# Linear attention over 16 images on one core: evictions ahead of the first exponential, statistics loads ahead of stores, one rounding and one load moved past the natural chunks, image 0 in a new order

## The chip, the cores and the metric

The kernel runs on 1 core of one Trainium2 chip. The metric is the device time of one execution in microseconds; lower is better. Five engines work side by side and meet only at semaphores: PE (TensorE, matrix products; its weight loads are listed as PEld), DVE (VectorE), ACT (ScalarE), POOL (GpSimd) and SP (SyncE), which here issues every DMA.

## The reference

`x` holds 16 images of 64 x 64 positions with 256 channels, in fp32. Each is normalized in 32 groups, goes through a linear attention whose keys get a softmax over the 4096 positions, and is added to the result.

```python
def _L0_conv_ref(x, W_qkv, W_out, b_out):
    b, h, w, c = x.shape
    n = h * w
    qkv = jnp.einsum('bhwc,cd->bhwd', x, W_qkv)
    q, k, v = jnp.split(qkv, 3, axis=-1)
    q = q.reshape(b, n, c).transpose(0, 2, 1)
    k = k.reshape(b, n, c).transpose(0, 2, 1)
    v = v.reshape(b, n, c).transpose(0, 2, 1)
    k = jax.nn.softmax(k, axis=-1)
    context = jnp.einsum('bdn,ben->bde', k, v)
    out = jnp.einsum('bde,bdn->ben', context, q)
    out = out.reshape(b, c, h, w).transpose(0, 2, 3, 1)
    return jnp.einsum('bhwc,cd->bhwd', out, W_out) + b_out

def _gn(v, G=32, eps=1e-5):
    B_, H_, W_, C_ = v.shape
    g = v.reshape(B_, H_, W_, G, C_ // G)
    m = jnp.mean(g, axis=(1, 2, 4), keepdims=True)
    s = jnp.var(g, axis=(1, 2, 4), keepdims=True)
    return ((g - m) / jnp.sqrt(s + eps)).reshape(v.shape)

x = x + _L0_conv_ref(_gn(x), L0_conv_W_qkv, L0_conv_W_out, L0_conv_b_out)
```

## The kernel before, in words

An image is cut into 8 chunks of 512 positions. Each chunk comes in twice: as `xt` with the channels on the partitions (the "transposed" chunks, `load_xt`) and as `x` with the positions on the partitions (the "natural" chunks, `load_x`). A third copy, `xs`, comes in 16 halves of 256 KB (`load_xs`) and only feeds the statistics of the normalization (`bn_half`, written `bn q` below for half q), two images ahead. Every fp32 operand of a product is split into a high part, rounded to fp32r, and a low part, the rest: ACT rounds (`xt_high`, `x_high`), and POOL subtracts (`xt_low`, `x_low`).

For each image PE makes keys, 8 chunks (`keys`, into the two halves of `ps_k`); ACT copies them out (`keys_out`, L747) and DVE keeps their running maximum (`key_maxes`, four L994 or L991 instructions a chunk). After chunks 0 to 3 and again after 4 to 7, `block_max` and `block_diag` bring the block's maxima into a diagonal, PE spreads it (`spread_max`, L506), and DVE subtracts it (`shift`, L1054). ACT makes the exponential twice (`exps`): rounded, L755, and exact, L761; `e_low` (L1061) is the difference. PE then gathers the context, chunk by chunk (`gather_high`, L542 and L544, needs `e_hi`, `x_hi` and `x_lo`; `gather_low`, L554, needs `e_lo` and frees the chunk's slots). `combine_u` and `combine_m` fold the context with the weights, and `emit` (L625, L634) makes the output, chunk by chunk in EMIT_ORDER (3, 4, 5, 6, 7, 0, 1, 2), position u, in two halves h. ACT adds the bias and writes `o_stage` (its `emit`, L795), and SP stores it.

A period of the loop works on two images: PE gathers and combines image b and makes the keys of image n = b + 1 between its emits (emit u, then keys u + 1). The order on every engine is written by hand, and each engine goes through its list in order: one waiting instruction holds all that follow. SP too has one list: its loads and stores are issued in the written order, each behind a wait for its slot, and all land through one queue. Two of these slots matter here. `o_stage` has 2, so ACT's emit of position u waits for the store of u - 2; and `ps_e` has one bank for each half, so PE's `emit(u + 1, h)` waits until ACT has taken (u, h). The first image has an order of its own, `first_gather` on DVE, and POOL makes the first POOL_LOW = 3 `e_low` of it (L398).

Of the kernel before, what the change touches and what calls it, by code (L numbers as in the profile page):

```python
# [25 lines left out]
XS_AFTER = {0: (4, 8), 2: (8, 12), 3: (12, 16)}  # L26

FIRST_XT = (8, 11, 15)
POOL_LOW = 3
# [5 lines left out]
def build(nc: bass.Bass, xt: bass.AP, xn: bass.AP, w: bass.AP, b_out: bass.AP, out: bass.AP):  # L35
# [11 lines left out]
    with ExitStack() as ctx:  # L47
# [232 lines left out]
        def _(sp):  # L280
# [45 lines left out]
            def period(b, parity, more, more2):  # L326
                for j in range(X_SLOTS, NCH):
# [13 lines left out]
                for u, j in enumerate(EMIT_ORDER):  # L341
                    if more2 or (more and j not in DOUBLED):
# [9 lines left out]
                    if more2 and u in XS_AFTER:  # L352
                        for q in range(*XS_AFTER[u]):
                            sp.wait_ge(bn_done, b * (NCH * CB) + 2 * NCH * CB + q - S_SLOTS + 1)
                            load_xs(b + 2, q)
# [8 lines left out]
        def _(pool):  # L364
# [61 lines left out]
            def period(b, parity, more, more2):  # L426
                n, np_ = b + 1, 1 - parity
                if more and b:
                    pool.wait_ge(var_parts_ready, n)
                pool.wait_ge(dm_ready, b + 1)  # L430
                if more:
                    xt_low(n, np_, 0)
                    if b:
                        rstd_of(n, np_)
                        scale_mean(n, np_)
                for j in range(HALF, NCH):
                    x_low(b, j)
                    if b == 0 and j == NCH - 2:
                        rstd_of(n, np_)
                        scale_mean(n, np_)  # L440
# [17 lines left out]
        def _(pe):  # L458
# [220 lines left out]
            def period(b, parity, more, more2):  # L679
                n, np_ = b + 1, 1 - parity  # L680
                gather_high(b, 0)
                if more and b:
                    stats_mean(n)
                gather_low(b, 0)
                gather_high(b, 1)
                if b == 0:
                    gather_low(b, 1)
                    gather_high(b, 2)
                spread_max(b, 1)
                if more and b:  # L690
                    stats_var(n)
                gather_low(b, 2 if b == 0 else 1)
                for j in range(3 if b == 0 else 2, NCH):
# [605 lines left out]
```

## Time and profile before

| | before |
|---|---|
| median of 3 runs | 1199.64 us (1195.49, 1199.64, 1200.19) |
| the profiled execution | 1202.58 us, its span 1200.6 us |
| PE busy | 1166.4 us (97%) |
| DVE busy | 931.0 us (78%) |
| ACT busy | 836.3 us (70%) |
| POOL busy | 627.0 us (52%) |
| mean DMA rate over the span | 222 GB/s |

The profiled execution took 2.9 us more than the median. The span runs from the first to the last instruction of the profiled execution. Rows of the timeline begin with start and duration in us; the idle time in brackets is what the engine waited before that instruction, with what ended it, and rows of one line close together are merged (x4 stands for four instructions, whose whole extent the duration is).

### The profile page before, as it was taken

To read this page: it belongs to the slowest core of one execution; us is meant where nothing else is said; L and a number is where in the kernel's file an instruction comes from. 1 tells how busy PE (TensorE), PEld (TensorE's weight loads), DVE (VectorE), ACT (ScalarE), POOL (GpSimd) and SP (SyncE) were. 2 spreads that over 40 slices of the span, in tenths; PEclk is the share of its full clock that TensorE was granted. 3 is DMA by queue.
4 is the path that set the end of the run, shared out by engine and by line. 5 is a ranking of instruction groups with operands and counts; after the bars stand their busy time and mean duration, and the time that the engine had idled before them with its cause. 6 is when DMAs were issued, how large, how long until landed. Compare 5 with 4: busy or idle time off the path is not lost.

```text
span 1200.6 us, 21468 instructions
## 1 busy us (share of the span) xinstructions
PE 1166.4 (97%) x8206; PEld 1089.3 (91%) x8206; DVE 931.0 (78%) x2008; ACT 836.3 (70%) x1146; POOL 627.0 (52%) x305
## 2 busy tenths in 40 slices
PE   4999999999999999999999999999999999999998
PEld 3889999989899898998989999899999989999996
DVE  6988779787796877878787797878869788796561
ACT  5667768677685776857777676776857768577764
POOL 7655563645656355553655636456463655536530
PEclk9999999999999999999999999999999999999999
DMA  8438666586766758657486665867657586573524
GB/s 318 163 134 315 228 216 236 179 296 214 258 212 202 263 188 280 228 201 250 165 316 228 215 232 179 303 212 261 214 199 271 179 295 227 198 254 119 190 84 162
DMA packets 107078, 266.70 MB, mean 222 GB/s; under 512 B 10208, under 2 KB 10208, under 8 KB 106976
## 3 DMA queue, kind: packets, MB, share of 16 engines
q1 hardware_dynamic: 106976, 265.33, 63.7%
q8 instruction: 65, 1.06, 0.4%
q14 instruction: 37, 0.30, 0.1%
HBM read 198.18 MB, written 67.11 MB: 221 GB/s over the span
## 4 chain that ended last, share of the span: by engine, by line
PE 82%; DMA 6%; DVE 4%; ACT 3%; issue 2%; POOL 1%; SPq 1%; DVEq 0%; ACTq 0%; POOLq 0%
PE ps_k L460 24%; PE ps_e L625 18%; PE ps_e L634 9%; PE ps_e L542 5%; PE ps_e L554 5%; PE ps_e L544 5%; DMA xs<-in_xt_dram 4%; PE ps_g L554 4%; PE ps_g L544 4%; PE ps_g L542 4%; PE ps_g L573 1%; PE ps_g L590 1%; DMA x_raw<-in_xn_dram 1%; DVE bn L922 1%; DVE e_raw L1054 1%
## 5 line engine op out<-in xcount | busy, mean ns | idle before, releaser
L387 POOL TENSOR_TENSOR xt_lo<-xt_raw,xt_hi 128x1024 fp32r<-128x1024 f32 x128 | 307.5, 2404 | 458.8 <-ACT xt_hi L738 194.1
L393 POOL TENSOR_TENSOR x_lo<-x_raw,x_hi 128x1024 fp32r<-128x1024 f32 x128 | 282.4, 2225 | 59.9 <-ACT x_hi L743 50.5
L994 DVE TENSOR_TENSOR mx<-ps_k,mx 128x256 f32<-128x256 f32 x480 | 203.1, 423 | 72.0 <-ACT e_raw L747 50.2
L795 ACT ACTIVATE o_stage<-ps_e,bias 128x512 f32<-128x512 f32 x253 | 168.8, 687 | 105.5 <-PE ps_e L634 101.5
L460 PE MATMUL ps_k<-wk_hi,xt_hi 128*128 128x256 f32 x1024 | 205.9, 283 | 1.4 <-DVE mx L994 1.2
L460 PE MATMUL ps_k<-wk_lo,xt_hi 128*128 128x256 f32 x1024 | 205.0, 282 | 0.0
L747 ACT ACTIVATE e_raw<-ps_k 128x512 f32<-128x512 f32 x256 | 141.2, 595 | 78.1 <-PE ps_k L460 78.1
L755 ACT ACTIVATE e_hi<-e_raw 128x1024 fp32r<-128x1024 f32 x128 | 134.8, 1053 | 67.2 <-DVE e_raw L1054 45.4
L922 DVE BATCH_NORM_STATS2 bn<-xs 128x6 f32<-128x512 f32 x240 | 153.8, 685 | 33.2 <-DMA xs<-in_xt_dram 31.9
L460 PEld LDWEIGHTS ps_k<-wk_hi,xt_hi 128*128 128x128 f32 x1024 | 164.3, 189 | 10.6 <-issue 2.4
L460 PE MATMUL ps_k<-wk_hi,xt_lo 128*128 128x256 f32 x1024 | 157.5, 282 | 0.0
L460 PEld LDWEIGHTS ps_k<-wk_lo,xt_hi 128*128 128x128 f32 x1024 | 157.1, 189 | 0.0
L625 PE MATMUL ps_e<-xt_hi,acc_hi 128*128 128x512 f32 x474 | 149.6, 397 | 4.6 <-ACT o_stage L795 4.5
L634 PE MATMUL ps_e<-xt_hi,u_lo 128*128 128x512 f32 x474 | 149.8, 397 | 0.0
L625 PE MATMUL ps_e<-xt_lo,acc_hi 128*128 128x512 f32 x474 | 149.1, 395 | 0.0
L743 ACT ACTIVATE x_hi<-x_raw 128x1024 fp32r<-128x1024 f32 x128 | 134.4, 1050 | 18.2 <-DMA x_raw<-in_xn_dram 18.2
L738 ACT ACTIVATE xt_hi<-xt_raw 128x1024 fp32r<-128x1024 f32 x128 | 135.1, 1055 | 3.8 <-DMA xt_raw<-in_xt_dram 3.7
L460 PEld LDWEIGHTS ps_k<-wk_hi,xt_lo 128*128 128x128 f32 x1024 | 137.2, 189 | 0.0
L542 PE MATMUL ps_e<-x_hi,e_hi 128*128 128x258 f32 x512 | 127.2, 286 | 2.6 <-POOL x_lo L393 2.5
L544 PE MATMUL ps_e<-x_lo,e_hi 128*128 128x256 f32 x512 | 126.5, 284 | 0.0
L542 PE MATMUL ps_g<-x_hi,e_hi 128*128 128x258 f32 x512 | 124.6, 282 | 0.0
L544 PE MATMUL ps_g<-x_lo,e_hi 128*128 128x256 f32 x512 | 124.5, 281 | 0.0
(147 smaller groups left out, 2027.6 us busy)
## 6 DMA issues: line engine op xcount, KB each, us to landing
xt_raw<-in_xt_dram SPq DMA_DIRECT2D x128, 512.0 KB, 4.6
x_raw<-in_xn_dram SPq DMA_DIRECT2D x128, 512.0 KB, 3.8
out_dram<-o_stage SPq DMA_DIRECT2D x127, 512.0 KB, 4.5
xs<-in_xt_dram SPq DMA_DIRECT2D x240, 256.0 KB, 5.0
w_setup<-in_w_dram SPq DMA_DIRECT2D x2, 256.0 KB, 9.7
out_dram<-o_stage SPq DMA_DIRECT2D x2, 256.0 KB, 2.0
wk<-in_w_dram SPq DMA_DIRECT2D x1, 256.0 KB, 10.0
wq_t<-in_w_dram SPq DMA_DIRECT2D x1, 256.0 KB, 11.0
```

What stands on the lines that cost most here:

```text
L387: nc.gpsimd.tensor_tensor(xt_lo[:, s], xt_raw[:, s], xt_hi[:, s].bitcast(F32), ALU.subtract).then_inc(xt_lo_ready, 1)
L393: nc.gpsimd.tensor_tensor(x_lo[:, s], x_raw[:, s], x_hi[:, s, :, 0:C].bitcast(F32), ALU.subtract).then_inc(x_lo_ready, 1)
L460: return nc.tensor.matmul(ps_k[:, j % 2, t // 2, (t % 2) * C:(t % 2 + 1) * C], (xt_hi, xt_lo)[xs_][:, slot(j, parity), c, t * P:(t + 1) * ...
L542: nc.tensor.matmul(ps_g[j // HALF][:, d, 0:C + 2], w_, x_hi[:, j % X_SLOTS, t, :], start=(j % HALF == 0 and t == 0), stop=False, skip_grou ...
L544: nc.tensor.matmul(ps_g[j // HALF][:, d, 0:C], w_, x_lo[:, j % X_SLOTS, t, :], start=False, stop=False, skip_group_check=True)
L625: nc.tensor.matmul(out_psum(b, u, h), hi[:, c, h * P:(h + 1) * P], x_[:, s, c, :], start=(n == 0 and c == 0), stop=False, skip_group_check ...
L634: last = nc.tensor.matmul(out_psum(b, u, h), lo[:, c, h * P:(h + 1) * P], xt_hi[:, s, c, :], start=False, stop=(c == CB - 1), skip_group_c ...
L738: nc.scalar.activation(xt_hi[:, s], xt_raw[:, s], ACT.Copy).then_inc(xt_hi_ready, 1)
L747: nc.scalar.activation(e_raw[:, j, 2 * h:2 * h + 2, :].rearrange("p t c -> p (t c)"), ps_k[:, j % 2, h, :], ACT.Copy).then_inc(k_out, 1)
L795: nc.scalar.activation(o_stage[:, u % O_SLOTS, h, :], src, ACT.Identity, bias=bias[:, h:h + 1]).then_inc(o_ready, 1)
L922: nc.vector.bn_stats(bn[:, q % CB, q // CB, :], xs[:, q % S_SLOTS, :]).then_inc(bn_done, 1)
L994: nc.vector.tensor_tensor(mx[:], tile, mx[:], ALU.max).then_inc(max_done, 1)
```

## The change

It only reorders: no instruction is added or left out, and one `e_low` of image 0 goes from POOL to DVE. Four parts belong to every period: (1) ACT takes the two output halves of position 4 ahead of the first exponentials of the next image; (2) SP issues the statistics loads ahead of the stores, and DVE takes two more of them ahead of the maxima of chunk 3, and three fewer between `block_diag` and the first `shift`; (3) ACT rounds transposed chunk 2 behind the natural chunks; (4) SP loads transposed chunk 2 of the next image behind natural chunks 4 and 5. The rest belongs to image 0.

```diff
-XS_AFTER = {0: (4, 8), 2: (8, 12), 3: (12, 16)}
-FIRST_XT = (8, 11, 15)
-POOL_LOW = 3
+XS_AHEAD = {0: (4, 8), 1: (8, 12), 2: (12, 14), 4: (14, 16)}
+FIRST_XT = (11, 13, 15)
+FIRST_X = (6, 7, 8, 9)
+POOL_LOW = 2
...
             for q in range(S_SLOTS, CB * NCH):
-                if q < 2 * X_SLOTS:
-                    load_x(0, q - X_SLOTS)
                 sp.wait_ge(bn_done, NCH * CB + q - S_SLOTS + 1)
                 load_xs(1, q)
+                if q in FIRST_X:
+                    load_x(0, FIRST_X.index(q))
...
                 for j in range(X_SLOTS, NCH):
                     sp.wait_ge(g_ps, b * NCH + (j - X_SLOTS + 1))
                     load_x(b, j)
+                    if more and b and j == X_SLOTS + 1:
+                        sp.wait_ge(e_ps, b * (CB * NCH))
+                        load_xt(n, 1 - parity, EMIT_ORDER[NCH - 1])
...
-                    if more2 or (more and j not in DOUBLED):
+                    if u < NCH - 1 and (more2 or (more and j not in DOUBLED)):
...
+                    if more2 and u in XS_AHEAD:
+                        for q in range(*XS_AHEAD[u]):
+                            sp.wait_ge(bn_done, b * (NCH * CB) + 2 * NCH * CB + q - S_SLOTS + 1)
+                            load_xs(b + 2, q)
                     if b == B - 1 and u == NCH - 1:
                         store_last()
                     elif not late(b, u, CB - 1):
                         store(b, u)
-                    if more2 and u in XS_AFTER:
...
+                if b == 0:
+                    pool.wait_ge(e_lo_ready, e_lo_count(0, HALF - 1))
...
                 for j in range(HALF, NCH):
+                    if b == 0 and j == NCH - 1:
+                        pool.wait_ge(var_parts_ready, 1)
                     x_low(b, j)
+                    if b == 0 and j == HALF + 1:
+                        xt_low(n, np_, 0)
...
+                def first_gather():
+                    gather(0, 0)
+                    gather_high(0, 1)
+                    gather_high(0, 2)
+                    gather_low(0, 1)
+                    spread_max(0, 1)
+                    gather_high(0, 3)
+                    gather_low(0, 2)
+                    gather_low(0, 3)
+                    gather(0, 4)
+                    stats_mean(1)
+                    gather(0, 5)
+                    gather_high(0, 6)
+                    stats_var(1)
+                    gather_low(0, 6)
+                    gather(0, 7)
...
             for j in range(X_SLOTS):
-                x_high(0, j)
                 keys_out(0, j, 0)
                 keys_out(0, j, 1)
+                x_high(0, j)
...
+                if b == 0:
+                    exps(0, 3)
+                    x_high(0, 4)
+                    xt_high(1, 1, 0)
+                    scales(0)
+                    for j in range(HALF, NCH):
+                        exp_high(0, j)
+                        if j < NCH - 1:
+                            x_high(0, j + 1)
+                        exp_exact(0, j)
+                    xt_high(1, 1, 1)
...
-                if more:
-                    xt_high(n, np_, 2)
                 for j in range(5, NCH):
                     x_high(b, j)
                     exps(b, j)
                 if more:
                     wk_high(n, np_)
+                    xt_high(n, np_, 2)
...
                 both_out(4)
+                emit(b, 4)
                 if more:
                     exps(n, 0)
-                emit(b, 4)
...
-            for q in range(1, 5):
+            for q in range(1, 7):
                 bn_half(1, q)
             for j in range(HALF):
                 key_maxes(0, j)
-                for q in ((5, 6), (7, 8), (9,), ())[j]:
+                for q in ((7, 8), (9, 10), (11,), ())[j]:
                     bn_half(1, q)
```

On SP, the part of a middle period that loads and stores beside the emits of positions 0 to 4 (`xt_raw` is a transposed chunk, `xs` a half for the statistics, `out_dram` a store). Before:

```order
L285 DMA xt_raw<-in_xt_dram 128x1024 [waits e_ps]
L304 DMA out_dram<-o_stage 128x2x512 [waits o_ready]
L294 DMA xs<-in_xt_dram 128x512 [waits bn_done] x4
L285 DMA xt_raw<-in_xt_dram 128x1024 [waits e_ps]
L304 DMA out_dram<-o_stage 128x2x512 [waits o_ready]
L285 DMA xt_raw<-in_xt_dram 128x1024 [waits e_ps]
L304 DMA out_dram<-o_stage 128x2x512 [waits o_ready]
L294 DMA xs<-in_xt_dram 128x512 [waits bn_done] x4
```

and now:

```order
L287 DMA xt_raw<-in_xt_dram 128x1024 [waits e_ps]
L296 DMA xs<-in_xt_dram 128x512 [waits bn_done] x4
L306 DMA out_dram<-o_stage 128x2x512 [waits o_ready]
L287 DMA xt_raw<-in_xt_dram 128x1024 [waits e_ps]
L296 DMA xs<-in_xt_dram 128x512 [waits bn_done] x4
L306 DMA out_dram<-o_stage 128x2x512 [waits o_ready]
L287 DMA xt_raw<-in_xt_dram 128x1024 [waits e_ps]
L296 DMA xs<-in_xt_dram 128x512 [waits bn_done] x2
```

The second four `xs` loads (q 8 to 11) have moved from behind the store of position 2 to ahead of that of position 1, and every store now stands behind loads that wait for DVE's statistics.

On DVE, a middle period from the maxima of chunk 2 of the next image to the first `shift` (`mx` is the running maximum, `bn` a statistics half, `e_raw<-e_raw,ps_g` the shift). Before:

```order
L922 BN_STATS bn<-xs 128x6 x4
L994 TENSOR_TENSOR mx<-ps_k,mx 128x256 x4
L922 BN_STATS bn<-xs 128x6 x4
L994 TENSOR_TENSOR mx<-ps_k,mx 128x256 x4
L1005 STREAM_TRANSPOSE turned<-mx 128x256
...
L1028 TENSOR_TENSOR u_hi<-eyes,m_parts 128x256
L922 BN_STATS bn<-xs 128x6 x4
L1054 TENSOR_TENSOR e_raw<-e_raw,ps_g 128x1024
```

and now:

```order
L968 BN_STATS bn<-xs 128x6 x4
L1040 TENSOR_TENSOR mx<-ps_k,mx 128x256 x4
L968 BN_STATS bn<-xs 128x6 x6
L1040 TENSOR_TENSOR mx<-ps_k,mx 128x256 x4
L1051 STREAM_TRANSPOSE turned<-mx 128x256
...
L1074 TENSOR_TENSOR u_hi<-eyes,m_parts 128x256
L968 BN_STATS bn<-xs 128x6
L1100 TENSOR_TENSOR e_raw<-e_raw,ps_g 128x1024
```

Two statistics halves moved ahead of the maxima of chunk 3, and one instead of four stands between the diagonal (`u_hi`) and the shift; one more now follows the maxima of chunk 4.

On DVE in image 0, from the block scales (`dm`) to the first `e_low` of the second block (`e_lo<-ps_k`). Before:

```order
L1038 TENSOR_TENSOR dm<-m_blk,m_all 32x16
L922 BN_STATS bn<-xs 128x6 x2
L1054 TENSOR_TENSOR e_raw<-e_raw,ps_k 128x1024
L1061 TENSOR_TENSOR e_lo<-e_raw,e_hi 128x1024
L922 BN_STATS bn<-xs 128x6 x2
...
L1054 TENSOR_TENSOR e_raw<-e_raw,ps_k 128x1024
L1061 TENSOR_TENSOR e_lo<-ps_k,e_hi 128x1024
```

and now:

```order
L1084 TENSOR_TENSOR dm<-m_blk,m_all 32x16
L1107 TENSOR_TENSOR e_lo<-e_raw,e_hi 128x1024 x2
L1100 TENSOR_TENSOR e_raw<-e_raw,ps_k 128x1024
L968 BN_STATS bn<-xs 128x6
L1100 TENSOR_TENSOR e_raw<-e_raw,ps_k 128x1024
L968 BN_STATS bn<-xs 128x6
...
L1107 TENSOR_TENSOR e_lo<-ps_k,e_hi 128x1024
```

Two statistics halves have left this place for the key stage, one `e_low` has come from POOL, and `take_first` (not shown) has gone behind the statistics and the `e_low` of chunk 6.

## Rows read from the trace of the kernel before

**Rows 1.** The page: busy time by engine.

```profile
PE 1166.4 (97%) x8206; PEld 1089.3 (91%) x8206; DVE 931.0 (78%) x2008; ACT 836.3 (70%) x1146; POOL 627.0 (52%) x305
```

**Rows 2.** Waits of PE's weight loads, 80 to 1150 us: released by, us, times, longest.

```profile
PEld ps_e L625 <- ACT o_stage L795: 6.2, 8, 1.8
PEld ps_e L542 <- issue: 3.1, 5, 1.0
```

**Rows 3.** Timeline, PE: start, duration; the statistics matmul, one of fifteen, once an image.

```profile
128.59 0.17 PE L517 MATMUL ps_k<-mean_parts,grp_r 128*128 128x4 f32 x1
...
566.63 0.17 PE L517 MATMUL ps_k<-mean_parts,grp_r 128*128 128x4 f32 x1
638.62 0.17 PE L517 MATMUL ps_k<-mean_parts,grp_r 128*128 128x4 f32 x1
...
1074.22 0.17 PE L517 MATMUL ps_k<-mean_parts,grp_r 128*128 128x4 f32 x1
```

**Rows 4.** Timeline of the image with the longest wait, DVE and PEld.

```profile
543.76 1.94 DVE L922 BATCH_NORM_STATS2 bn<-xs 128x6 f32<-128x512 f32 x3 [1.70 <-DMA xs<-in_xt_dram]
546.65 1.20 DVE L1054 TENSOR_TENSOR e_raw<-e_raw,ps_g 128x1024 f32<-128x1024 f32 x1
550.52 0.30 PEld L625 LDWEIGHTS ps_e<-xt_hi,acc_hi 128*128 128x128 f32 x2 [1.78 <-ACT o_stage L795]
```

**Rows 5.** The same place in the next image, DVE, ACT, PEld.

```profile
611.58 1.87 DVE L994 TENSOR_TENSOR mx<-ps_k,mx 128x256 f32<-128x256 f32 x4 [1.97 <-ACT e_raw L747]
615.54 0.42 DVE L1028 TENSOR_TENSOR u_hi<-eyes,m_parts 128x256 fp32r<-128x256 f32 x1
616.73 0.19 PEld L506 LDWEIGHTS ps_g<-u_hi,one_r 128*128 128x128 f32 x1
621.69 1.24 ACT L795 ACTIVATE o_stage<-ps_e,bias 128x512 f32<-128x512 f32 x2
622.49 0.31 PEld L625 LDWEIGHTS ps_e<-xt_hi,acc_hi 128*128 128x128 f32 x2
```

**Rows 6.** Ahead of it: DVE, SP, and one window (end: PEclk, DMA share, GB/s).

```profile
607.09 2.52 DVE L922 BATCH_NORM_STATS2 bn<-xs 128x6 f32<-128x512 f32 x4 [2.06 <-DMA xs<-in_xt_dram]
605.78 0.33 SPq L285 DMA_DIRECT2D xt_raw<-in_xt_dram  x1
609.00:610.00 1.00, 1.00 (x11) 1.00 (x10) 0.61 (x1) 0.27 (x1) 0.89 (x1) 1.00 1.07 399
```

**Rows 7.** The page, DMA issues: KB each, median us from issue to landing.

```profile
out_dram<-o_stage SPq DMA_DIRECT2D x127, 512.0 KB, 4.5
xs<-in_xt_dram SPq DMA_DIRECT2D x240, 256.0 KB, 5.0
```

**Rows 8.** A late natural chunk: ACT and POOL.

```profile
1007.56 1.06 ACT L743 ACTIVATE x_hi<-x_raw 128x1024 fp32r<-128x1024 f32 x1 [2.10 <-DMA x_raw<-in_xn_dram]
1010.52 1.04 ACT L738 ACTIVATE xt_hi<-xt_raw 128x1024 fp32r<-128x1024 f32 x1
1012.59 2.21 POOL L393 TENSOR_TENSOR x_lo<-x_raw,x_hi 128x1024 fp32r<-128x1024 f32 x1 [1.69 <-ACT x_hi L743]
```

**Rows 9.** ACT ahead of `acc_high`, a middle image.

```profile
515.34 0.91 ACT L777 ACTIVATE acc_hi<-acc,rz 128x256 fp32r<-128x256 f32 x2 [4.28 <-DVE acc L1085]
```

**Rows 10.** Image 0, DVE.

```profile
28.70 0.69 DVE L922 BATCH_NORM_STATS2 bn<-xs 128x6 f32<-128x512 f32 x1 [1.27 <-DMA xs<-in_xt_dram]
39.59 0.16 DVE L1023 TENSOR_TENSOR m_parts<-m_blk,m_parts 32x8 fp32r<-32x8 f32 x1
54.86 1.44 DVE L1023 TENSOR_TENSOR m_parts<-m_blk,m_parts 32x8 fp32r<-32x8 f32 x1
74.50 1.22 DVE L1061 TENSOR_TENSOR e_lo<-ps_k,e_hi 128x1024 fp32r<-128x1024 f32 x1 [1.62 <-ACT ps_k L761]
```

**Rows 11.** Windows of image 0: the columns of rows 6, PE's busy time first.

```profile
22.00:79.00 57.00, 52.15 (x401) 50.40 (x401) 48.67 (x108) 36.81 (x49) 39.26 (x19) 0.97 0.56 191
64.00:66.00 2.00, 2.00 (x11) 2.00 (x11) 1.90 (x6) 1.93 (x2) 1.55 (x1) 0.50 0.93 290
```

More of the change, by code:

```diff
@@ L680, in period, with gather_steps @@
                 n, np_ = b + 1, 1 - parity
[L681 to L685, printed above, removed]
-                if b == 0:
[L687 to L693, printed above, removed]
-                    gather(b, j)
-                    if b == 0 and j == 3:
-                        stats_mean(n)
-                    if b == 0 and j == 4:
-                        stats_var(n)
+                def first_gather():
[14 more added lines that the diff above has]
+                    gather(0, 7)
+                def gather_steps():
+                    gather_high(b, 0)
+                    if more:
+                        stats_mean(n)
+                    gather_low(b, 0)
+                    gather_high(b, 1)
+                    spread_max(b, 1)
+                    if more:
+                        stats_var(n)
+                    gather_low(b, 1)
+                    for j in range(2, NCH):
+                        gather(b, j)
+                if b == 0:
+                    first_gather()
+                else:
+                    gather_steps()
                 if more:
@@ L761, in exps @@
                 nc.scalar.activation(to, e_raw[:, j].rearrange("p t c -> p (t c)"), ACT.Exp).then_inc(e_ready, 1)
+            def exps(b, j):
+                exp_high(b, j)
+                exp_exact(b, j)
             def scales(b):
@@ L833, in period @@
                 n, np_ = b + 1, 1 - parity
-                if more:
-                    xt_high(n, np_, 0)
-                exps(b, 3)
-                if more:
-                    xt_high(n, np_, 1)
-                x_high(b, 4)
-                scales(b)
-                exps(b, 4)
-                if more:
-                    xt_high(n, np_, 2)
-                for j in range(5, NCH):
-                    x_high(b, j)
-                    exps(b, j)
+                if b == 0:
+                    exps(0, 3)
[8 more added lines that the diff above has]
+                    xt_high(1, 1, 1)
+                else:
+                    if more:
+                        xt_high(n, np_, 0)
+                    exps(b, 3)
+                    if more:
+                        xt_high(n, np_, 1)
+                    x_high(b, 4)
+                    scales(b)
+                    exps(b, 4)
+                    for j in range(5, NCH):
+                        x_high(b, j)
+                        exps(b, j)
                 if more:
                     wk_high(n, np_)
+                    xt_high(n, np_, 2)
                 def both_out(j):
@@ L1164, in _ @@
             key_maxes(0, 4)
[L1165 removed]
+            bn_half(1, 13)
             key_maxes(0, 5)
@@ L1176, in first_gather @@
                 block_scales(0)
-                bn_half(1, 12)
-                bn_half(1, 13)
+                e_low(0, 2)
+                e_low(0, 3)
                 shift(0, 4)
-                e_low(0, 3)
                 bn_half(1, 14)
+                shift(0, 5)
                 bn_half(1, 15)
                 bn_sum(1)
-                shift(0, 5)
                 e_low(0, 4)
+                shift(0, 6)
+                shift(0, 7)
+                e_low(0, 5)
                 mean_of(1, 1)
+                e_low(0, 6)
+                var_of(1)
                 spread_scales(0)
                 take_first(0)
-                shift(0, 6)
-                var_of(1)
-                e_low(0, 5)
-                shift(0, 7)
-                e_low(0, 6)
                 e_low(0, 7)
@@ L1262, in period @@
                 e_low(n, 1)
-                bn_halves(14, 16)
+                bn_halves(14, 15)
                 shift(n, 3)
                 key_maxes(n, 6)
+                bn_halves(15, 16)
                 if more2:
```

28 lines of the change are left out of this document (13 added, 15 removed).

## The prediction

> **What bounds the kernel now.** I read the page first. PE works for 1166.4 of the 1200.6 us of the span [rows 1], so at most the 34 us in which it doesn't can be won, and only by edits that end one of its waits. DVE stands at 78%, ACT at 70%, and a shorter list on them is worth nothing by itself. The second view is the waits of PE's weight loads in the steady part, 80 to 1150 us [rows 2]. Two entries there have to do with what the change moves: 6.2 us in 8 waits of the first emission product for ACT's eviction, and 3.1 us in 5 waits ahead of `gather_high`, put down to "issue". Third, the length of an image, from one statistics product to another [rows 3]: 1074.22 less 128.59 is 945.63 us over thirteen images, 72.74 each, while the image that starts at 566.63 takes 71.99. If all thirteen took that, 9.8 us would go; the two waits make 9.3 of it. This is what the loop has to give, and the two views agree on it.
>
> The timeline of the worst image tells where the first wait comes from [rows 4]. DVE waits 1.70 us for an `xs` half, then makes the statistics, and `shift(0)` can start only at 546.65, because these statistics stand ahead of it in DVE's list. ACT's list has the two exponentials of chunk 0 ahead of its emission of position 4. So ACT idles until the shift, makes both exponentials, and PE, which wants the bank of `ps_e` for position 5, waits 1.78 us. One image later no half is late: ACT's evictions start at 621.69 and take 0.62 us each, so the first is out at 622.31, and PE takes the bank at 622.49 with no wait [rows 5]. The order has almost no slack there, and whether an image loses time depends on when the halves land.
>
> The second wait begins at a natural chunk that lands late [rows 8]: ACT waits 2.10 us for it, then comes the next natural chunk's turn only behind the rounding of transposed chunk 2 (1.04 us at 1010.52), POOL's `x_lo` waits 1.69 us for ACT, and PE's product starts late, by up to 1.0 us [rows 2].
>
> **Part 1, the emission of position 4 ahead of the exponentials, with the statistics loads.** Once ACT's emission no longer stands behind the exponentials, a late shift doesn't hold PE's bank. What it holds instead is the exponentials, and PE needs these only in the next gather. `shift(0)` itself comes earlier by three statistics (2.63 us in [rows 5] is four of them before; 0.69 a piece, so about 2.0), and the late half of [rows 4] is asked for one store sooner. The whole 6.2 us of [rows 2] should go: −6.2. The lower bound of the gain is what the eight waits would leave if ACT were late for another reason; I see none in these rows and take the whole.
>
> **Part 2, two more statistics ahead of the maxima of chunk 3.** This can cost. In the image of [rows 5] DVE starts these maxima at 611.58, after 1.97 us of idleness for ACT's copy. The diagonal that they end in is ready at 615.54 + 0.42 = 615.96, and PE loads it at 616.73: 0.77 us of slack. The statistics of halves 8 and 9 must now be done before 611.58. Their loads follow the transposed load issued at 605.78 [rows 6], half 9 at about 606.5; with the median 5.0 us from issue to landing [rows 7] it would land at 611.5 and its statistics (0.69) end at 612.2, 0.6 us late and inside the slack. At 399 GB/s a half takes 256 KB / 399 = 0.66 us and a store 1.3 [rows 6], so with one store less ahead of it than the median load has it would end at about 611.5, not late at all. In some images the queue is slower: a half a microsecond to a microsecond later gives PE 0.2 to 0.7 us of waiting at `spread_max`. I put 1.0 us for all fourteen images, with 0 as the lower bound and 14 × 0.5 = 7 as the upper.
>
> The stores now stand behind the halves. Store 1 waits until the last of four loads is issued, which waits for the statistics that end at 607.09 + 2.52 = 609.61 [rows 6]; at the median 4.5 us [rows 7] it lands at 614.1, ACT's first half into its slot is out 0.62 us later, at 614.7, and PE wants position 4 behind `spread_max` of 616.73 [rows 5]. Two microseconds cover it: 0, and the price without the cover is in the rivals.
>
> **Part 3, the rounding and the load of transposed chunk 2.** The load goes behind two natural chunks: one transfer of 512 KB less ahead of the late chunk, 1.3 us at the rate of [rows 6] against the 2.10 us by which it is late [rows 8]. The rounding moves to the place where ACT waits 4.28 us for `acc` [rows 9], so its 1.04 us costs nothing there; were that idle time gone, it would be 1.04 an image. Together 2.3 us go from a chain that made PE 1.0 us late at its worst: −3.1, all of the second entry of [rows 2]. Less is possible, if some of these waits ("issue" names no releaser) have another cause; that end is 0.
>
> **Part 4, image 0.** From 22 to 79 us PE is busy 52.15 of 57.00 us and its granted clock is 0.97 in the mean [rows 11]: 4.9 us of waits, and 57 × 0.03 = 1.7 us of clock, nearly all of it behind the waits at 60 to 64 us, after which the clock was granted at half, 1.2 instead of 2.4 GHz, for the whole of 64 to 66. DVE sets this stretch. In the stage of the keys its list gets two statistics more ahead of the first block (2 × 0.63 = 1.26, a quarter of the 2.52 of [rows 6] each), and one of these loads is likely to be late as half 6 was, 1.27 us [rows 10], since they are worked off faster than four slots are filled: +2.53. In the gather stage two statistics leave (−1.26) and the `e_low` that comes from POOL adds 1.22, as the one at 74.50. `m_parts` took 1.44 us at 54.86 and 0.16 at 39.59, for the same operands [rows 10], in a stretch in which POOL made its `e_low`; POOL now starts no work before DVE's `e_low` of chunk 3 has ended: −1.28. And DVE's wait of 1.62 us at 74.50 for ACT goes, as ACT now rounds ahead: −1.62. The sum is 2.53 − 1.26 + 1.22 − 1.28 − 1.62 = −0.4. The bounds are wide: +3.8 if nothing but the additions counts (2.53 + 1.22), −6 if the waits and the clock of [rows 11] go nearly whole.
>
> On the 1.44 us the Trainium skill has a rule: "SBUF — State Buffer", section "SBUF: two separate sides", has DVE and GpSimd share one pair of ports, which a DVE operation with two SBUF inputs and a GpSimd operation that reads SBUF take for a whole instruction each, in turn. The trace agrees, with 1.44 beside 0.16. By the rule POOL's work, now placed beside DVE's shifts and `e_low`s, would be blocked by them in turn, and what is won at `m_parts` could be lost again at another operation of DVE: the 1.28 us would stay, and image 0 would be +0.9 instead of −0.4.
>
> In the last keys stage no statistics leave DVE's list, and ACT's exponentials come behind two evictions of 0.62 [rows 5], up to 1.2 us later; as they wait for the shift in part of it I take +0.3, with bounds of 0 and 1.2.
>
> **The sum.** −6.2 − 3.1 + 1.0 − 0.4 + 0.3 = −8.4, from the profiled execution's 1202.58: **1194.2 us**. That execution was 2.9 us above the median of 1199.64, so against the median it is −5.4 us, 0.45% less. About 0.5%, 6.0 us, is also what a measurement of this kernel can tell from no change, so faster means under 1193.6 and slower over 1205.6.
>
> **The rivals.**
> - *Image 0 comes out much better.* DVE no longer makes PE wait in the gather, so that the clock stays at its upper level; of the 6.6 us of [rows 11] some 1.5 are left. Then image 0 gives 5.1 instead of 0.4: 1194.2 − 4.7 = 1189.5. For it speaks that the whole list of image 0 was rewritten for every engine; against it, that DVE's work there is not less.
> - *A new wait takes the old one's place.* Half 8 or 9 lands late as a rule, the maxima of chunk 3 slip by 1.3 us, beyond the slack of 0.77, and PE waits 0.5 us at `spread_max` in all fourteen images: 1194.2 − 1.0 + 7 = 1200.2. The half that was 1.70 us late in [rows 4] speaks for it; that it is now asked for one store sooner, against.
> - *The stores are late: slower.* Each store waits behind halves that wait for statistics. From the point at which store 1 lands more than 2.0 us later than I have it, past 616, PE waits for ACT at position 3 or 4, and the late stores push the transposed loads behind them too. At 1 us in each of fourteen images it is 1194.2 + 14 = 1208.2. Against it stands that the four loads ahead take only 4 × 0.66 = 2.6 us, and were to be moved sooner or later anyway.
> - *The clock.* PE is held in the key stage of image 0 by the two statistics put ahead, as it was at 60 to 64 us, and the clock falls there too. The half level over some 4 us costs 2.0: 1196.2. "TensorE: Matmul & The Clock Gate", Part 1, of the Trainium skill says that a PE left idle goes back to the lower level; the trace agrees with 0.50 at 64 to 66 us behind the waits.
>
> **How the numbers follow.** The forecast has 0.48 and a range of its own of 1191.5 to 1197.0 (part 3 short by 3 us upward, or part 2 at 0 and 1.5 better in image 0 downward); the better image 0 has 0.17, the new wait 0.22, the late stores 0.08, the clock 0.05. The range of 1188.5 to 1200.5 takes in all but the late stores and the outer parts of the better image 0 and of the new wait. Faster by over 0.5% are the whole better image 0 and about half of the forecast, whose own range the bound of 1193.6 halves: 0.42. Slower are the late stores and the tail of the new wait at its upper bound: 0.11. The rest, 0.47, is within.
>
> **What the profile after would show.** Part 1 is right if the waits of PE's emission product for ACT's `o_stage` fall under 1 us in all, and the shift starts some 2 us sooner after the diagonal. Part 3 is right if the waits ahead of `gather_high` go from 3.1 to under 1. The price of part 2 would stand as waits of PE for the diagonal (`ps_g` released by DVE `u_hi`), with DVE waiting for `xs` right ahead of the maxima of chunk 3. Image 0 shows in PE's busy time and clock from 22 to 79 us. Late stores would show as waits of ACT's emission for the DMA of `out_dram`. The prediction would be wrong if the mean image stayed near 72.7 us, or if it fell but image 0 gave as much back.

## The result

The changed kernel is slower: 1207.74 us in the median of 6 runs (1205.23 to 1209.72) against 1197.15 us of before (6 runs, 1195.49 to 1200.19). The ratio is 1.0083, with a 95% interval of [1.0064, 1.0102]. The forecast was 1194.2 us in a range of 1188.5 to 1200.5.

The page of the changed kernel, busy time by engine:

```profile
PE 1166.4 (97%) x8206; PEld 1088.0 (90%) x8206; DVE 933.8 (77%) x2009; ACT 838.3 (70%) x1146; POOL 629.2 (52%) x304
```

PE's work is the same 1166.4 us as in [rows 1]. What grew is its idle time. The waits of PE's weight loads, 80 to 1150 us, changed kernel (released by, us, times, longest):

```profile
PEld ps_g L519 <- DVE u_hi L1074: 10.8, 14, 1.7
...
PEld ps_e L555 <- issue: 2.0, 4, 0.8
PEld ps_k L540 <- DVE var_parts L1006: 0.7, 2, 0.4
```

Against [rows 2] the wait of the emission for ACT's `o_stage` has gone altogether, the one ahead of `gather_high` has shrunk from 3.1 to 2.0 (what went lay in the last two images, 1.4 us of it; in the thirteen between it is 2.0 against 1.8), and a new one stands first: PE waits for the diagonal `u_hi` in each of the fourteen images with statistics, 0.40 to 1.69 us. The timeline of PE in the changed kernel, the statistics product once an image:

```profile
129.85 0.17 PE L530 MATMUL ps_k<-mean_parts,grp_r 128*128 128x4 f32 x1
...
567.25 0.17 PE L530 MATMUL ps_k<-mean_parts,grp_r 128*128 128x4 f32 x1
640.13 0.17 PE L530 MATMUL ps_k<-mean_parts,grp_r 128*128 128x4 f32 x1
...
1080.72 0.17 PE L530 MATMUL ps_k<-mean_parts,grp_r 128*128 128x4 f32 x1
```

Thirteen images take 950.87 us, 73.14 each, against 72.74 in [rows 3]; the one from 567.25 takes 72.88, and its counterpart of before took 71.99. That image starts 0.62 us later than its counterpart (567.25 against 566.63), so 0.62 is to be taken off a time of it before it is compared with [rows 5] or [rows 6]. Its timeline (start, duration; SP, DVE, ACT and PEld apart in the trace):

```profile
604.36 0.40 SPq L306 DMA_DIRECT2D out_dram<-o_stage  x1
606.41 0.33 SPq L287 DMA_DIRECT2D xt_raw<-in_xt_dram  x1
606.79 3.58 SPq L296 DMA_DIRECT2D xs<-in_xt_dram  x4
610.41 0.43 SPq L306 DMA_DIRECT2D out_dram<-o_stage  x1
...
605.95 1.42 DVE L968 BATCH_NORM_STATS2 bn<-xs 128x6 f32<-128x512 f32 x2 [0.30 <-DMA xs<-in_xt_dram]
608.73 1.29 DVE L968 BATCH_NORM_STATS2 bn<-xs 128x6 f32<-128x512 f32 x2 [1.36 <-DMA xs<-in_xt_dram]
612.41 1.50 DVE L968 BATCH_NORM_STATS2 bn<-xs 128x6 f32<-128x512 f32 x2 [2.40 <-DMA xs<-in_xt_dram]
613.82 1.85 DVE L1040 TENSOR_TENSOR mx<-ps_k,mx 128x256 f32<-128x256 f32 x4
617.77 0.42 DVE L1074 TENSOR_TENSOR u_hi<-eyes,m_parts 128x256 fp32r<-128x256 f32 x1
...
611.74 1.08 ACT L776 ACTIVATE e_raw<-ps_k 128x512 f32<-128x512 f32 x2
...
618.25 0.18 PEld L519 LDWEIGHTS ps_g<-u_hi,one_r 128*128 128x128 f32 x1 [0.74 <-DVE u_hi L1074]
```

The six statistics come in three pairs: 4 and 5, 6 and 7, and the two that were moved, 8 and 9. DVE waits 2.40 us for half 8, ends statistic 9 at 613.91, and the maxima of chunk 3 start then and not, as in [rows 5], when ACT's copy is there; ACT had ended that copy at 612.82. In all fourteen images the maxima start just as statistic 9 ends, 0.8 to 2.1 us behind the end of ACT's copy; before, they started 0.5 us ahead of that end, with the copy's first half, in all fourteen. The load of half 9 (tile `xs`, 607.35 to 607.5 us):

```profile
L296 SPq DMA_DIRECT2D xs<-in_xt_dram x1: 437/437/437, 607.4 to 607.4; - x1
...
DMA to landing us min/median/max: 5.8/5.8/5.8
```

It was issued at 607.4 and landed at 613.2. Statistic 5, which frees its slot, had ended at 605.95 + 1.42 = 607.37. In thirteen of the fourteen images half 9 is issued 0.03 to 0.04 us after the end of that image's statistic 5 (in one 0.15), and it takes 4.3 to 6.6 us to land, 5.2 in the mean. The stores moved too. ACT's waits for stores in the changed kernel, 80 to 1150 us:

```profile
ACT o_stage L830 <- DMA out_dram<-o_stage: 80.3, 38, 3.8
```

Before, ACT waited 0.3 us for stores in that stretch. Now it waits 80.3 us, and yet no wait of PE for `o_stage` is in PE's list: these 80 us are idle time of an engine that has it to spare.

### The profile page after: what moved, and what is told of

Its sections match the earlier page's. It is cut to its first block, busy times and chain, and to the rows that moved or that the text cites. A ratio compares the mean times of both kernels' runs of the same rounds, so it can differ in the third digit from the quotient of the medians.

```text
span 1205.6 us, 21469 instructions
## 1 busy us (share of the span) xinstructions
PE 1166.4 (97%) x8206; PEld 1088.0 (90%) x8206; DVE 933.8 (77%) x2009; ACT 838.3 (70%) x1146; POOL 629.2 (52%) x304
## 4 chain that ended last, share of the span: by engine, by line
PE 66%; DMA 14%; DVE 13%; issue 3%; ACT 2%; POOL 1%; SPq 0%; DVEq 0%; ACTq 0%; POOLq 0%
PE ps_k L473 17%; PE ps_e L638 12%; DMA xs<-in_xt_dram 12%; PE ps_e L647 6%; PE ps_g L567 5%; PE ps_e L567 4%; PE ps_e L555 4%; PE ps_e L557 4%; PE ps_g L557 4%; PE ps_g L555 4%; DVE mx L1040 4%; DVE bn L968 3%; PE ps_g L586 1%; PE ps_g L603 1%; DMA out_dram<-o_stage 1%
## 5 line engine op out<-in xcount | busy, mean ns | idle before, releaser
L394 POOL TENSOR_TENSOR xt_lo<-xt_raw,xt_hi 128x1024 fp32r<-128x1024 f32 x128 | 313.6, 2452 | 460.0 <-ACT xt_hi L767 189.1
L1040 DVE TENSOR_TENSOR mx<-ps_k,mx 128x256 f32<-128x256 f32 x480 | 203.1, 423 | 35.5 <-ACT e_raw L776 13.2
L968 DVE BATCH_NORM_STATS2 bn<-xs 128x6 f32<-128x512 f32 x240 | 157.9, 686 | 65.1 <-DMA xs<-in_xt_dram 64.0
## 6 DMA issues: line engine op xcount, KB each, us to landing
w_setup<-in_w_dram SPq DMA_DIRECT2D x2, 256.0 KB, 10.2
wk<-in_w_dram SPq DMA_DIRECT2D x1, 256.0 KB, 10.8
```

Of the source, the lines that this page charges most:

```text
L394: nc.gpsimd.tensor_tensor(xt_lo[:, s], xt_raw[:, s], xt_hi[:, s].bitcast(F32), ALU.subtract).then_inc(xt_lo_ready, 1)
L968: nc.vector.bn_stats(bn[:, q % CB, q // CB, :], xs[:, q % S_SLOTS, :]).then_inc(bn_done, 1)
L1040: nc.vector.tensor_tensor(mx[:], tile, mx[:], ALU.max).then_inc(max_done, 1)
```

## The experiments

Ratios are to runs of the kernel before on the same chip, whose medians were 1197.86, 1198.73 and 1197.99 us in the three groups (e1 to e4, e5 to e8, e9 to e12).

**e1.** The changed kernel, on DVE alone:

```diff
-                bn_halves(4, 10)
+                bn_halves(4, 8)
                 key_maxes(n, 3)
...
-                bn_halves(10, 11)
+                bn_halves(8, 11)
                 shift(n, 0)
```

> The changed kernel with one edit on DVE: the statistics of halves 8 and 9 stand behind block_diag again. Theory 1 (these two statistics, waiting for their halves, hold the maxima of chunk 3): PE's waits for the diagonal fall from 10.8 us to under 1 us in 80 to 1150 us, and the time goes from 1207.7 to 1197 to 1199. Theory 2 (the stores, now behind the halves, come late, so that ACT copies the keys of chunk 3 late and the maxima wait for that): the maxima move forward only as far as ACT's copy lets them, over 5 us of the waits stay, and the time stays above 1203.

Measured: 1231.61 us (1229.42 to 1233.53), 1.0284 [1.0267, 1.03]. Neither time was met. The wait for the diagonal did go, as theory 1 says, but others came. PE's waits in e1, 80 to 1150 us:

```profile
PEld ps_k L473 <- ACT xt_hi L767: 11.1, 14, 0.8
PEld ps_k L540 <- DVE var_parts L1006: 9.0, 14, 0.9
PEld ps_k L473 <- POOL xt_lo L394: 8.8, 15, 0.6
PEld ps_e L638 <- ACT o_stage L830: 8.3, 13, 2.2
```

and SP's list at the place, e1:

```profile
623.45 0.47 SPq L287 DMA_DIRECT2D xt_raw<-in_xt_dram  x1
630.06 0.93 SPq L296 DMA_DIRECT2D xs<-in_xt_dram  x2
631.04 0.43 SPq L306 DMA_DIRECT2D out_dram<-o_stage  x1
```

SP issues nothing from 623.92 to 630.06: halves 12 and 13 wait for the slots of 8 and 9, whose statistics now come behind `block_diag`, and the store of position 2 stands behind them. ACT waited 118.1 us for stores instead of 80.3. So the two parts of the change hang together: with the loads of 12 and 13 ahead of that store, statistics 8 and 9 have to be ahead of the maxima.

**e2.** The changed kernel, on SP alone: the block that loads the statistics halves stands behind the store instead of ahead of it, in each position.

```diff
-                    if more2 and u in XS_AHEAD:
...
                     if b == B - 1 and u == NCH - 1:
                         store_last()
                     elif not late(b, u, CB - 1):
                         store(b, u)
+                    if more2 and u in XS_AHEAD:
...
```

> The changed kernel with one edit on SP: in each position the store is issued ahead of the statistics loads, the rest stays. Theory 1: halves 8 and 9 land one store (some 1.3 us) later, the statistics ahead of the maxima of chunk 3 end later by as much, and PE's waits for the diagonal grow from 10.8 us by 0.5 to 1.3 us an image, 7 to 18 us in all: 1214 to 1225. Theory 2: ACT's 80 us of waits for stores go, and with them most of PE's waits: about 1199.

Measured: 1228.97 us (1224.09 to 1232.0), 1.0252 [1.023, 1.0275]. PE's waits in e2:

```profile
PEld ps_g L519 <- DVE u_hi L1074: 27.8, 14, 3.5
```

One store more ahead of the halves adds 17.0 us to the wait for the diagonal, 1.2 an image, within what theory 1 gave; ACT's wait for stores is gone, and PE won nothing by it. In the mean of the fourteen images half 9 lands 0.5 us slower (5.7 against 5.2), and its issue stands 4.0 us ahead of the end of ACT's copy instead of 4.8: together the 1.3 us that one store was taken for. Theory 2 falls. The total is above my number by 4 us and more: here ACT also waits 31.4 us for transposed chunks, which come later too, and I didn't divide the remainder further.

**e3.** The kernel before with the swap alone.

```diff
                 both_out(4)
+                emit(b, 4)
                 if more:
                     exps(n, 0)
-                emit(b, 4)
```

> The kernel before with one part alone: ACT takes position 4 out ahead of the exponentials of chunk 0. If the wait of PE's emission for ACT is as large in the median run as in the profiled one, 6.2 us go: 1191 to 1192 from the median of 1197.2. If that profiled execution (1202.6) was a bad one, and most of these waits are absent from a usual run, 1 to 3 us go: 1194 to 1196. The rival that the exponentials, now 1.2 us later, hold DVE and then PE: 1199 or more.

Measured: 1199.07 us (12 runs, 1194.8 to 1204.41), 1.0013 [0.9997, 1.003]: no difference that can be told. No wait for ACT's `o_stage` is in the list of 80 to 1150 us, as expected, and the profiled run took 1196.48. But the runs spread over 9.6 us. Three waits of PE in the profiled run belong to one image, the only steady one that took over 73 us (74.21):

```profile
632.82 0.19 PEld L517 LDWEIGHTS ps_k<-mean_parts,grp_r 128*128 128x128 f32 x1 [0.54 <-DVE mx L994]
636.35 0.18 PEld L506 LDWEIGHTS ps_k<-u_hi,one_r 128*128 128x128 f32 x1 [0.48 <-DVE u_hi L1028]
637.95 0.19 PEld L527 LDWEIGHTS ps_k<-var_parts,grp_r 128*128 128x128 f32 x1 [1.41 <-DVE var_parts L960]
```

Here DVE is late at the start of the gather, and PE waits three times. In the trace it is DVE's list of the key stage that runs over: a late shift has later exponentials behind it (now behind the emission too), and `e_low` and the last maxima follow these. I read this, and have no run for it alone.

**e4.** The kernel before with the chunk 2 part alone (its diff is that of the change for `load_xt(n, 1 - parity, EMIT_ORDER[NCH - 1])` and `xt_high(n, np_, 2)`).

> The kernel before with one part alone: transposed chunk 2 is loaded behind natural chunks 4 and 5, and rounded behind the natural chunks. By the step of the prediction 3.1 us of waits ahead of gather_high go: 1194 from 1197.2. If the usual run has few of them, or their cause is another: 1196 to 1198, and waits of over 1.5 us stay in the trace.

Measured: 1196.84 us (1195.77 to 1199.52), 0.9995 [0.9987, 1.0004]. PE's waits, 80 to 1150 us:

```profile
PEld ps_e L629 <- ACT o_stage L799: 3.7, 5, 1.3
...
PEld ps_e L546 <- issue: 0.7, 1, 0.7
```

The edit does what it should, 0.7 us are left ahead of `gather_high`, but the time falls by 1 us at most. The traces show a price in image 0 that nobody had put down. With the rounding of chunk 2 gone from between them, ACT makes two natural chunks closer together, POOL subtracts both without a pause, and a small operation of DVE for the statistics takes 2.14 us beside it, where it took 0.16 in before and in e12:

```profile
58.55 5.31 POOL L397 TENSOR_TENSOR x_lo<-x_raw,x_hi 128x1024 fp32r<-128x1024 f32 x2
...
61.74 2.14 DVE L937 TENSOR_TENSOR mean_parts<-mv,mean_parts 128x2 fp32r<-128x2 f32 x1
```

It is 2.13 to 2.14 us in e4, e8 and e9, the three kernels with this part and the old order of image 0, and 0.16 in before, e12, e3 and e6. The first statistics product comes at 64.0 to 64.2 us in the three and at 62.0 to 63.0 in the four. From the last statistics product to the end the three take 124.9 to 125.0 us and the four 126.0 to 126.4. So this part wins over 1 us in the last two images and loses about as much in image 0.

**e5.** The edit of e1, and one number on SP:

```diff
-XS_AHEAD = {0: (4, 8), 1: (8, 12), 2: (12, 14), 4: (14, 16)}
+XS_AHEAD = {0: (4, 8), 1: (8, 12), 3: (12, 14), 4: (14, 16)}
```

> The changed kernel with statistics 8 and 9 behind block_diag, as in the first experiment, and also the loads of halves 12 and 13, which wait for them, moved on SP from ahead of the store of position 2 to ahead of that of position 3. If the first experiment was slow (1231.6) because that store stood behind loads that wait for statistics made only behind the diagonal, ACT's 118 us of waits for stores fall back to 80 or less, PE's waits for the diagonal stay near 0, and the time is 1197 to 1201. If it was slow because the statistics delay the shift and all behind it, the time stays over 1220.

Measured: 1196.18 us (12 runs, 1194.01 to 1199.77), 0.9983 [0.9973, 0.9994]: 11.6 us less than the changed kernel, and slightly under the kernel before. No wait for the diagonal of a block with statistics (`ps_g`) is left; the one of 1.2 us (`ps_k`) belongs to the last image and is there in before too. PE's waits, 80 to 1150 us, and DVE's row for the maxima of chunk 3 of a middle image:

```profile
PEld ps_k L519 <- DVE u_hi L1074: 1.2, 1, 1.2
PEld ps_e L555 <- issue: 0.3, 1, 0.3
...
607.14 1.87 DVE L1040 TENSOR_TENSOR mx<-ps_k,mx 128x256 f32<-128x256 f32 x4 [2.60 <-ACT e_raw L776]
```

DVE is idle for 2.60 us ahead of the maxima and waits for ACT, as in [rows 5]. All thirteen steady images take 71.9 to 72.3 us. ACT still waits 70.5 us for stores; these don't keep the kernel from being fast.

**e6.** The kernel before with part 2 alone, SP's and DVE's side.

```diff
-XS_AFTER = {0: (4, 8), 2: (8, 12), 3: (12, 16)}
+XS_AHEAD = {0: (4, 8), 1: (8, 12), 2: (12, 14), 4: (14, 16)}
...
-                bn_halves(4, 8)
+                bn_halves(4, 10)
                 key_maxes(n, 3)
...
```

> The kernel before with part 2 alone: statistics loads ahead of the stores, and two statistics ahead of the maxima of chunk 3. If this part alone costs what the changed kernel loses, PE's waits for the diagonal are 9 to 12 us in 80 to 1150 us, those of the emission for ACT's eviction go (the shift comes earlier), and the time is 1203 to 1207. If the loss needs the other parts too: 1199 or less.

Measured: 1208.06 us (1206.46 to 1213.34), 1.0085 [1.0065, 1.0105], as slow as the whole change. PE's waits, 80 to 1150 us:

```profile
PEld ps_g L506 <- DVE u_hi L1028: 13.2, 14, 1.8
PEld ps_e L542 <- issue: 3.1, 6, 1.0
...
PEld ps_e L625 <- ACT o_stage L795: 0.2, 1, 0.2
```

The emission's wait is nearly gone without the swap. The earlier shift may have done that, or PE, held at the diagonal, comes later for the bank; this run doesn't separate them.

**e7.** The kernel before with image 0's new order alone (all edits of the change that stand under `b == 0` or ahead of the loop).

> The kernel before with image 0's new order alone. By the prediction's sum 0.4 us less than before, 1197.5; if the changed kernel's first 130 us tell its price (the second statistics product 1.3 us later than before, with the clock better there by 1.7 us in the mean), 1198 to 1200; the rival that it is much better, 1193 to 1195.

Measured: 1201.01 us (12 runs, 1197.08 to 1203.26), 1.0019 [1.0007, 1.0032]: some 2.3 us more. PE's longest entry, 20 to 82 us (2.4 in before):

```profile
PEld ps_k L469 <- issue: 5.3, 4, 2.0
```

**e8.** The swap and the chunk 2 part on the kernel before.

> The kernel before with the swap of the emission and the exponentials and with the chunk 2 part, without the rest. If the two waits of the steady part are independent, both go, and the time is 1193 to 1195. The swap alone swung between 1194.8 and 1204.4 from run to run: if that comes from natural chunks landing late, this kernel is narrower; if it comes from elsewhere, it swings as much and its median is 1197 to 1199.

Measured: 1198.21 us (12 runs, 1194.11 to 1208.55), 1.0008 [0.9986, 1.0031]. It swings as e3 does, over 14 us, with the lowest runs at 1194, though no wait of PE ahead of `gather_high` is left in its profiled run; so those waits aren't what swings. In its profiled run (1197.55) twelve of thirteen images take 72.0 to 72.2 us, and one 75.71. In that one PE waits 0.38, 0.48 and 1.42 us at the three places of e3. These are 2.3 of the 3.7 us by which it is longer; behind them the clock was granted at half, 1.2 of 2.4 GHz, for the whole of 136 to 138 us (length, PE, PEld, DVE, ACT, POOL busy; clock, DMA share, GB/s):

```profile
136.00:138.00 2.00, 2.00 (x12) 2.00 (x11) 1.97 (x4) 0.80 (x1) 2.00 (x2) 0.50 0.00 0
```

**e9.** The kernel of e5 with image 0 in the order of before.

> The kernel of the fifth experiment with image 0 in the order of before, so that it has the swap, the chunk 2 part and the statistics loads ahead of stores 0, 1, 3 and 4, with statistics 8 and 9 behind block_diag. The fifth took 1196.2 and image 0's new order alone cost 2.3 (1201.0 to 1198.7): if these add up, 1193.9. If image 0's new order is hidden or paid back in that kernel, 1196 or more. The steady images should take 72.0 to 72.3 us each.

Measured: 1195.37 us (12 runs, 1193.65 to 1196.88), 0.9977 [0.9968, 0.9986]. It is the steady part that I would keep, and its runs lie within 3.2 us, where those of e8, which lacks only the statistics part, spread over 14. The sum of 1193.9 wasn't met. Each against the runs of before on its own chip, e5 and e9 are both 2.6 us faster, so between these two image 0's new order costs nothing that can be told. Their profiled runs agree: the second statistics product comes at 129.70 in e5 and at 129.85 in e9. The reason is in e4: the old order of image 0 with the chunk 2 part isn't what before has, it costs 1.3 us more there (128.59 in before and in e12).

**e10.** The changed kernel with one statistic ahead of the maxima of chunk 3.

```diff
-                bn_halves(4, 10)
+                bn_halves(4, 9)
...
-XS_AHEAD = {0: (4, 8), 1: (8, 12), 2: (12, 14), 4: (14, 16)}
+XS_AHEAD = {0: (4, 8), 1: (8, 12), 2: (12, 13), 3: (13, 14), 4: (14, 16)}
```

> The changed kernel with one statistic (half 8) instead of two ahead of the maxima of chunk 3, and of the loads only half 12 ahead of the store of position 2. If the wait is set by when the last half ahead of the maxima lands and is worked off, it is shorter by one half's transfer and one statistic (0.66 + 0.69 = 1.3 us), which is more than 13 of the 14 waits for the diagonal (0.40 to 1.69 us): less than 1.5 us of them is left, and the time is 1197 to 1199. If one statistic ahead already costs (any wait for a half there passes on), 5 us or more stay and the time is 1202 or more.

Measured: 1198.25 us (12 runs, 1196.88 to 1202.05), 1.0007 [0.9996, 1.0018]. The waits for the diagonal:

```profile
PEld ps_g L519 <- DVE u_hi L1074: 4.4, 7, 1.1
```

The time is in the band of the first alternative, the waits are between both: half of the images still wait. The price is graded, 0 with none, 4.4 with one, 10.8 with two.

**e11.** The kernel of e5 with image 0's keys stage as before and its gather stage as in the change, with `bn_half(1, 12)` and `bn_half(1, 13)` ahead of `bn_half(1, 14)` there.

> The kernel of the ninth experiment with only the second half of image 0's new order: the gather stage as in the changed kernel (with statistics 12 and 13 in it), the stage of the keys as before. If the new order loses in the stage of the keys (PE's waits there 5.3 us in the image 0 experiment against 2.4) and gains in the gather stage, this is the fastest, 1192 to 1193.5. If the two additional statistics in the gather stage take the gain, it is as the ninth or slower, 1194 to 1196.

Measured: 1194.86 us (11 runs, 1193.48 to 1196.64), 0.9972 [0.9963, 0.9982], the lowest median of all. Against e9 it is 0.5 us less, with intervals that lie over each other, so which half of image 0's order wins stays unsettled.

**e12.** The kernel before, unchanged.

> The kernel before, profiled again. The profiled execution on which the prediction rests took 1202.6 us, above all 29 timed runs (1195.5 to 1201.0). If its waits are those of a bad execution, the waits for ACT's eviction and ahead of gather_high are well below 9.3 us here, 3 to 6, at a time of 1196 to 1199.

Measured: 1197.16 us (8 runs), the profiled one 1196.55. PE's waits, 80 to 1150 us:

```profile
PEld ps_e L542 <- issue: 2.6, 6, 0.9
PEld ps_e L625 <- ACT o_stage L795: 1.2, 1, 1.2
...
1068.22 0.17 PE L517 MATMUL ps_k<-mean_parts,grp_r 128*128 128x4 f32 x1
```

These are the two entries of [rows 2], 3.8 us together instead of 9.3. The last statistics product is at 1068.22 and the second again at 128.59, so thirteen images take 939.63 us, 72.28 each.

## Why the prediction was wrong

**The step that failed is part 2**, "I put 1.0 us for all fourteen images". It was 10.8 us, or 13.2 when alone (e6). The chain was told rightly, and so was the slack of 0.77 us, but not when half 9 is there. The prediction had its load issued at 606.5, right behind the transposed load, landing 5.0 us later and its statistic ended at 612.2, some 0.2 us inside the slack. On the same axis (0.62 us off the changed kernel's times) it was issued at 606.8, landed 5.8 us later, and its statistic ended at 613.3. The maxima start 1.6 us later than in [rows 5], ACT's copy itself is there 0.2 later, and PE waits 0.74. In this image it is the transfer that is long. Over all fourteen it is more the issue: half 9 is issued 4.80 us ahead of the end of ACT's copy in the mean, where the prediction had 5.54, and takes 5.23 us where it had 5.0. These 0.74 and 0.23 us, less the 0.15 that was to spare, make 0.8 us, and PE waits 0.77 in the mean.

The issue is late because of the slot. Half 9 takes the slot of half 5, and SP must wait until DVE has made statistic 5, in every one of the fourteen images. With four slots the eighth and ninth half can't run ahead of the fourth and fifth, and the prediction had followed the queue and not the slot. A kernel with a fifth slot wasn't run. e2 and e10 show the size from both sides, one transfer later and one half less.

**The rival "a new wait takes the old one's place" is what happened.** Its mechanism and sign were right. Its 0.5 us an image was 0.77 in the mean, and its 1200.2 was too low by the other terms below too.

**The sum, term by term.** Against the trace that it was made from the forecast was −8.4 us, and the span of the changed kernel is 5.0 longer (1205.6 us), so the forecast was 13.4 too low. Part 2 is 9.8 of them (10.8 for 1.0). Part 3 is 2.0: 1.1 of the 3.1 us went and not all, so the sign that it was to be known by, under 1, wasn't met. Image 0 is 1.1: the second statistics product is 1.26 us later, of which 0.53 is image 1's wait for the diagonal, so image 0 costs 0.7 and not −0.4. A wait of 0.7 for `var_parts` wasn't in the sum, and the end gave 0.4 more than was put down. Part 1's 6.2 us went (in e6 nearly all of them go without the swap), and its other sign came too: the first `shift` starts 0.52 us after the diagonal, against 2.3 to 4.6 before. These make 13.2 of 13.4.

**The gains of parts 1 and 3 were those of one bad execution.** The profiled execution of 1202.58 lies above all 34 runs of before that stand beside e9 to e12 (1195.98 to 1201.69). e12 at 1196.55 has 3.8 us in the two entries, and in the usual run there was little more to win. That moves the forecast less than it seems: what was too much in the waits was also too much in the 1202.58, and e9, which has no price of part 2, took 1195.37, near 1194.2. It does make the announced gain of 5.4 against the median too large. Nor did the two views of [rows 2] and [rows 3] agree as the prediction says: 1.4 of the 9.3 us lie behind 1074.22, outside its thirteen images. Each edit did remove its wait (e3, e4), and neither is faster by more than can be measured. Against e12 the changed kernel's span is 11.0 us longer: 1.3 up to the second statistics product, 11.2 in thirteen images (waits 10.2 for the diagonal, 0.7 for `var_parts`, 0.7 more ahead of `gather_high`, 1.2 less for the emission: 10.4, and 0.8 not assigned), and 1.5 less from there to the end.

**Part 1's margin, costed at nothing, wasn't nothing.** By themselves the swapped exponentials make the time swing (e3, e8). With the statistics part beside it, in the form of e5 and e9, it doesn't. Why is not shown.

**The late stores came, and PE didn't wait for them.** Store 1 was issued at 610.41, on the prediction's axis 609.8 and so nearly as forecast, but took 5.9 us to land and not 4.5: 615.7, just short of the 616 from which the rival counted. ACT waited 80.3 us for stores in all. e5 has 70.5 of these and is fast.

**What I hadn't seen at all** is that the two edits of part 2 are coupled (e1): take the statistics back alone and it costs 34 us more than before.

**Image 0** was given −0.4. The changed kernel's timeline, DVE, image 0:

```profile
31.25 0.70 DVE L968 BATCH_NORM_STATS2 bn<-xs 128x6 f32<-128x512 f32 x1 [1.94 <-DMA xs<-in_xt_dram]
42.87 0.16 DVE L1069 TENSOR_TENSOR m_parts<-m_blk,m_parts 32x8 fp32r<-32x8 f32 x1
58.15 0.16 DVE L1069 TENSOR_TENSOR m_parts<-m_blk,m_parts 32x8 fp32r<-32x8 f32 x1
65.62 1.15 DVE L980 TENSOR_TENSOR mean_parts<-mv,mean_parts 128x2 fp32r<-128x2 f32 x1
```

`m_parts` of the first block is at 42.87 against 39.59 in [rows 10]: the stage of the keys costs 3.28 where I had 2.53, because not one but several halves are late, as the one of 1.94 us. `m_parts` of the second block, 1.44 us in [rows 10], takes 0.16 again as predicted, but `mean_parts` takes 1.15 at 65.62, beside a POOL subtraction that runs from 64.55 to 66.75, and ends with it: what was won at one was lost at the other. In the Trainium skill, "SBUF — State Buffer", section "SBUF: two separate sides", the shared pair of ports is held for a whole instruction, by a DVE operation with two SBUF inputs or by a GpSimd operation that reads SBUF, while the other waits. The trace agrees at both places, and in e4 (2.14 us), and the branch of it that the prediction mentioned, that the loss only moves, is the one that came; it had given +0.9 for it, and 0.7 was measured. That 0.7 is with a clock of 1.00 from 22 to 79 us instead of 0.97, some 1.7 us better by the prediction's own estimate; the waits grew by more. So the engines don't meet "only at semaphores", as the section on the chip says: POOL's subtraction holds up DVE's operation with no semaphore between them.

## What to carry to other kernels

A load that runs ahead is bounded by its slot: before work is moved ahead of something that matters, follow the buffer back to the step that frees it, and take the latency of that place in the queue and not a median. Times of two traces are compared from the same step of the same image, and not from the start of the program. Waits in the steady part that differ from image to image should be read from two executions before they are subtracted, and from one that lies at the median. Where SP's list is in order, a load put ahead of a store ties the store to whoever frees that load's slot; move both or neither.

## What was unexpected

The granted clock was not the same for the same order of image 0. In the changed kernel PE waited 2.93 us at 33.84 and the window of 22 to 79 us still shows 1.00, with PE busy 49.30 of 57.00 us; it stays at 1.00 even behind 66 to 68 us, in which PE was busy 0.04 of 2.00 us. In e7 the clock fell behind the same stretch, in which PE was busy 0.33 of 2.00 us, to about its lower level, 1.2 of 2.4 GHz. Windows of the changed kernel and then of e7 (start:end, length, PE, PEld, DVE, ACT, POOL busy; clock, DMA share, GB/s):

```profile
22.00:79.00 57.00, 49.30 (x393) 47.57 (x393) 48.19 (x105) 36.84 (x49) 33.69 (x18) 1.00 0.58 199
66.00:68.00 2.00, 0.04 (x1) 0.04 (x1) 2.00 (x3) 1.37 (x3) 2.00 (x2) 1.00 0.88 202
68.00:70.00 2.00, 2.00 (x17) 2.00 (x18) 2.00 (x2) 1.90 (x2) 2.00 (x2) 1.00 1.01 386
```

```profile
66.00:68.00 2.00, 0.33 (x3) 0.13 (x2) 1.97 (x3) 1.77 (x2) 2.00 (x2) 1.00 0.69 240
68.00:70.00 2.00, 1.60 (x7) 1.60 (x8) 2.00 (x3) 1.52 (x2) 2.00 (x2) 0.62 0.99 378
70.00:72.00 2.00, 2.00 (x12) 2.00 (x11) 1.96 (x4) 1.74 (x3) 1.68 (x1) 0.53 0.58 181
```

That is an estimate of 0.38 × 2 + 0.47 × 2 = 1.7 us of clock which one execution pays and another doesn't. It isn't what makes image 0's new order cost 2.3 us in e7 and nothing between e5 and e9: e5's profiled execution shows 0.97 from 22 to 79 us, as e7's does, and the old order that e9 sets against it has a price of its own, the 2.14 us of e4.
